# Graph layer kernel, the rows' stage: edge keys in four slices a group in place of one lump

## The chip, the core and the metric

The kernel runs on one core of one Trainium2 chip. Its engines run beside each other, each from its own instruction stream, and meet only at semaphores: PE (TensorE) multiplies and transposes into PSUM, DVE (VectorE) and ACT (ScalarE) do elementwise work, POOL (GpSimd) does some adds and issues indirect DMAs, SP issues plain DMAs. The metric is device time in microseconds (us). Three runs of the kernel before give a median of 2010.76 us, from 2009.63 to 2011.68.

## What is computed

One layer of a graph transformer on 6250 rows of 256 numbers: a two-layer graph convolution over 200000 edges plus self-loops, a linear attention ("mix") and a slice-token attention ("ffn"). Cut to what this case touches:

```python
edge_index = jnp.stack([src, dst])          # 200000 edges, sorted by dst, plus self-loops
xn = _layernorm(x)
x = x + gnn(xn, edge_index, W1, b1, W2, b2) + mix(xn[None], W_qkv, b_qkv, W_mo, b_mo)[0]
# in mix: q, k, v = split(xn @ W_qkv + b_qkv); q, k centred; q2 = q*q; k2 = k*k
# k2 = l2_normalize(k2 / (sum(k2) + 1e-7), over rows); q2 = l2_normalize(q2 / (sum(q2) + 1e-7), over columns)
x = x + ffn(_layernorm(x)[None], ...)[0]
```

## The kernel before

The rows are cut into T = 49 tiles of 128. The edges, sorted by their target row, are cut into windows of two target rows each. A window has up to 128 edge slots. A later stage builds the adjacency matrix from "keys": for each edge slot, `key_lo` holds the source row's place in its tile (source modulo 128) and `key_hi` holds the source's tile and which of the window's two rows the edge ends in.

The change lies in the **rows' stage** (lines 581 to 919), which runs from about 70 to 290 us. It walks over the 49 tiles, and for tile t:

- SP loads the rows of x (L637) and stores two transposed results (L640, L645).
- DVE, in its turn t, does in this order: `norm(t+1)` (L695 reciprocal, L699 normalised rows, L702 their f16 half), `stats(t+2)` (L687, L689, L690), `over_norm(t-2)` (L727, L729, L731, L733), `over_sums(t-1)` (L717, L719, L721), `halves(t+1)` (L707) and, in some turns, `edge_keys` (L673 to L682).
- PE, in its turn t: `project(t)` (L785, L787), `turn(t+1)`, which transposes the normalised rows (L776) and, in 28 turns, a piece of the keys first (`turn_keys`, L764), and `gather(t-2)` (L795, and L802, which transposes what L733 made).
- ACT, in its turn t: `low_keys` in some turns (L899), `norms(t-2)` (L877, L880, L883), `std(t+2)` (L856), `keep(t+1)` (L863), `squares(t)` (L872), `store_keys` in 28 turns (L905), `turned(t-3)` (L889).
- POOL, in its turn t: for the first 28 tiles one indirect DMA that gathers the sources of a quarter group's edges (L832), then an add of the k4 rows (L846), which waits for ACT's L883.

The keys come in G = 7 groups of WPS = 4 window rows each (112 partitions x 4 x 128 slots). Before, `edge_keys(g)` handles a whole group, 112x512, in one go, at the end of DVE's turns 10, 14, ..., 34 (`KEYS_LAG` = 10, each fourth tile). It takes five instructions: L673 the low seven bits, L674 which slots lie beyond the window's edges, L678 the shift by seven bits, L679 adding 1024 for slots beyond, L682 the high key. `low_keys(g)` on ACT turns the low bits into floats one tile later. `keyl` and `keyh` have two buffers each. PE transposes the keys in 28 turns from tile 13 on (`KEYS_TURN` = 13), and `parts_made`, `keys_made` and `keyl_ready` count the steps.

The order on each engine is the order in which these functions are called; no scheduler changes it. L699 waits, beside its own inputs, for a ring buffer of four that PE's L795 frees (`kx_done`), L764 and L776 wait for L699 (`xn_ready`), and L802 waits for L733 (`q2f_ready`).

Of the kernel before, what the change touches and what calls it, by code (L numbers as in the profile page):

```python
# [5 lines left out]
ALU = mybir.AluOpType  # L6
# [32 lines left out]
def gps_layer(nc, x, src, dst, W1, b1, W2, b2, W_qkv, b_qkv, W_mo, b_mo,  # L39
# [45 lines left out]
    with ExitStack() as life:  # L85
# [496 lines left out]
        with ExitStack() as stage:  # L582
# [8 lines left out]
            first = take([GW, G, WPS])  # L591
            second = take([GW, G, WPS, CAP])
            srcg = take([GW, G, WPS, CAP], I32)
            beyond = take([GW, WPS, CAP])
            src_lo = take([GW, 2, WPS, CAP], I32)
            keyl = take([GW, 2, WPS, CAP])
            keyh = take([GW, 2, WPS, CAP])
            take = carve(big_f[:, 0:KEYS_AT])
            x_in = take([P, RING, C])
            xn = take([P, RING, C + 2])  # L600
# [12 lines left out]
            nq = take([P, RING])  # L613
            fq = take([P, RING])
            before_sources = (16 * G, 16 * G, 0)
            KEYS_LAG, KEYS_TURN = 10, 13
            KEY_PARTS = 4 * G
            assert KEYS_TURN + KEY_PARTS < T and WPS == 4
            x_loaded = [sem(f"x_loaded{b}") for b in range(RING)]
# [35 lines left out]
            def _(dve):  # L655
# [7 lines left out]
                v.tensor_scalar(dun[:, :], dinv[:, :], 1.0 / SH, None, ALU.mult).then_inc(dinv_ready, 1)  # L663
                dve.wait_ge(dinv_ready, 2)

                def edge_keys(g):

                    r = g % 2
                    dve.wait_ge(gathered[g % 3], before_sources[g % 3] + 16 * WPS * (g // 3 + 1))
                    if g >= 2:  # L670
                        dve.wait_ge(keyl_ready, g - 1)
                        dve.wait_ge(xn_turned, KEYS_TURN + WPS * (g - 2) + WPS)
                    v.tensor_scalar(src_lo[:, r], srcg[:, g], P - 1, None, ALU.bitwise_and).then_inc(parts_made, 1)  # L673
                    v.tensor_tensor(beyond, slot.rearrange("p (o s) -> p o s", o=1).to_broadcast([GW, WPS, CAP]),  # L674
                                    many[:, g].rearrange("p (w o) -> p w o", o=1).to_broadcast([GW, WPS, CAP]), ALU.is_ge
                                    ).then_inc(parts_made, 1)
                    dve.wait_ge(parts_made, 4 * g + 2)
                    v.tensor_scalar(srcg[:, g], srcg[:, g], 7, None, ALU.logical_shift_right).then_inc(parts_made, 1)  # L678
                    v.scalar_tensor_tensor(out=second[:, g], in0=beyond, scalar=1024.0, in1=second[:, g],  # L679
                                           op0=ALU.mult, op1=ALU.add).then_inc(parts_made, 1)  # L680
                    dve.wait_ge(parts_made, 4 * g + 4)
                    v.scalar_tensor_tensor(out=keyh[:, r], in0=srcg[:, g], scalar=float(WIN), in1=second[:, g],  # L682
                                           op0=ALU.mult, op1=ALU.add).then_inc(keys_made, 1)

                def stats(t, b, u):
# [67 lines left out]
            def _(pe):  # L753
                te = nc.tensor

                def turn_keys(n, bank):

                    g, high, pair = n // WPS, n % WPS // 2, n % 2
                    if high:
                        pe.wait_ge(keys_made, g + 1)  # L760
                    else:
                        pe.wait_ge(keyl_ready, g + 1)
                    for j in range(2):
                        te.transpose(ps[:, bank, C + j * GW:C + (j + 1) * GW],  # L764
                                     (keyh if high else keyl)[:, g % 2, 2 * pair + j, :], ident[0:GW, 0:GW])

                def turn(t, b):
                    pe.wait_ge(xn_ready, t + 1)
# [55 lines left out]
            @block.gpsimd  # L824
            def _(pool):
                g = nc.gpsimd
                g.memset(k4_sum, 0.0).then_inc(k4_zeroed, 1)
                pool.wait_ge(k4_zeroed, 1)

                def gather_sources(g, j):  # L830

                    pool.indirect_dma_start(  # L832
                        out=srcg[:, g, j, :], out_offset=None, in_=src_dram.rearrange("(e a) -> e a", a=1),
                        in_offset=bass.IndirectOffsetOnAxis(ap=wlo[:, g, j:j + 1], axis=0)).then_inc(gathered[g % 3], 16)

                pool.wait_ge(src_padded, 32)

                def tile(t, b, u):
                    if t < WPS * G:
                        if t % WPS == 0 and t // WPS >= 3:  # L840
                            pool.wait_ge(parts_made, 4 * (t // WPS - 3) + 1)
                        gather_sources(t // WPS, t % WPS)
                    pool.wait_ge(k4_ready, 2 * t + 2)
                    if reached(t, 1):
                        pool.wait_ge(k4_added, t)
                    g.tensor_tensor(k4_sum[0:rows(t), :], k4_sum[0:rows(t), :], k4[0:rows(t), b, :], ALU.add).then_inc(k4_added, 1)  # L846

                pipeline(tile, T, RING)

            @block.scalar  # L850
            def _(act):
# [41 lines left out]

                def low_keys(g):

                    act.wait_ge(parts_made, 4 * g + 1)
                    if g >= 2:
                        act.wait_ge(xn_turned, KEYS_TURN + WPS * (g - 2) + 2)
                    a.copy(keyl[:, g % 2], src_lo[:, g % 2]).then_inc(keyl_ready, 1)  # L899

                def store_keys(t, b):

# [4 lines left out]
                           ps[:, 3 * (b % 2), C:C + 2 * GW].rearrange("p (j w) -> p j w", w=GW)).then_inc(keys_stored, 1)  # L907

                def tile(t, b, u):
                    if reached(t, KEYS_LAG + 1) and (t - KEYS_LAG - 1) % WPS == 0 and (t - KEYS_LAG - 1) // WPS < G:  # L910
                        low_keys((t - KEYS_LAG - 1) // WPS)
# [103 lines left out]
        def sum_edges(layer, halves, scratch, un):  # L1015
# [6 lines left out]
            with ExitStack() as stage:  # L1022
                block = stage.enter_context(nc.Block())

                @block.vector
                def _(dve):
                    nc.vector.tensor_tensor(acc[0:NT], halves[0:NT, :, 0:C], halves[0:NT, :, C:2 * C], ALU.add)
                    nc.vector.memset(key_lo[:, :], 0.0).then_inc(e_wide, 1)
# [953 lines left out]
```

## Time and profile before

| What | us |
|---|---|
| median of three runs | 2010.76 |
| the profiled execution's own time | 2019.06 |
| its span in the profile | 2017.1 |
| PE busy over the span | 1894.1 (94%) |
| DVE busy | 1185.0 (59%) |
| ACT busy | 852.7 (42%) |
| POOL busy | 300.0 (15%) |
| first and last start of L785, one for each of the 49 tiles | 75.5 and 280.7 |

The profile lists each instruction with its start, its duration, its engine, its line, and what it writes and reads by shape. Time in brackets is idle time of the engine just before it, and behind the arrow stands who released it. The start-to-start distance of two neighbours on an engine can be shorter than the first one's duration, because neighbours overlap. PEclk is the granted clock of TensorE as a share of full speed.

### The profile page before, as it was taken

How to read it: one execution, taken by the hardware profiler on the slowest of the kernel's cores; microseconds unless marked ns; L12 is line 12 of the kernel's file. 1: busy time of each engine (PE TensorE's matmuls, PEld its weight loads, DVE VectorE, ACT ScalarE, POOL GpSimd, SP SyncE). 2: the span in 40 equal slices, each digit the busy share in tenths (PEclk: the TensorE clock that was granted, in tenths of full speed). 3: DMA queues.
4: the chain of work that ended last, by engine and by line, in shares of the span. 5: the costliest groups of instructions: out<-in, count | busy, mean ns of one | idle time of the engine just before them, and what ended most of it. 6: DMA issues, size and time to landing. Idle time of an engine off the chain costs nothing. (4 is left out here: it accounts for less than half of the span.)

```text
span 2017.1 us, 45282 instructions
## 1 busy us (share of the span) xinstructions
PE 1894.1 (94%) x18843; PEld 1415.6 (70%) x18843; DVE 1185.0 (59%) x2748; ACT 852.7 (42%) x1970; POOL 300.0 (15%) x417
## 2 busy tenths in 40 slices
PE   3598989999999999999979999999999999999598
PEld 3254555555555555555559999999999999998476
DVE  6788887666666666666605555555555555555322
ACT  1577765665656665666602222222222222222100
POOL 3133110000000000000021111111111111111033
PEclk7698999999999999999989999999999999999599
DMA  3133322223232222223254444444444444442087
GB/s 97 51 108 94 93 74 104 121 97 129 97 129 97 122 104 109 117 97 129 96 187 142 144 144 144 144 140 144 143 143 143 144 143 143 142 142 78 13 269 241
DMA packets 92702, 252.13 MB, mean 125 GB/s; under 512 B 14143, under 2 KB 59347, under 8 KB 79939
## 3 DMA queue, kind: packets, MB, share of 16 engines
q1 hardware_dynamic: 69225, 218.83, 30.4%
q10 hardware_dynamic: 21096, 25.65, 3.6%
q0 software_dynamic: 2176, 4.75, 0.9%
q8 instruction: 150, 2.46, 0.5%
q14 instruction: 55, 0.44, 0.1%
HBM read 131.99 MB, written 118.02 MB: 124 GB/s over the span
## 5 line engine op out<-in xcount | busy, mean ns | idle before, releaser
L1392 PE MATMUL ps<-hs,at 128*128 128x512 f16 x2401 | 669.8, 379 | 0.3 <-POOL at L1209 0.3
L1611 PE MATMUL ps<-at,big 128*128 128x128 f16 x9604 | 576.8, 219 | 7.0 <-DMA at<-at_scratch 7.0
L1611 PEld LDWEIGHTS ps<-at,big 128*128 128x128 f16 x9604 | 555.7, 98 | 34.6 <-issue 8.4
L1448 ACT CAST at<-ps 128x392 f16<-128x392 f32 x784 | 375.0, 486 | 289.5 <-PE ps L1353 274.1
L1353 PE MATMUL ps<-big 128*128 128x98 f16 x3136 | 471.6, 208 | 8.1 <-DVE big L1293 8.1
L1353 PEld LDWEIGHTS ps<-big 128*128 128x128 f16 x3136 | 297.8, 98 | 142.6 <-DVE big L1293 9.7
L1392 PEld LDWEIGHTS ps<-hs,at 128*128 128x128 f16 x2401 | 230.1, 97 | 149.0 <-issue 1.8
L1293 DVE TENSOR_TENSOR big<-iota_lo,key_lo 128x1024 f16<-128x1024 f16 x392 | 268.2, 684 | 0.0
L1293 DVE TENSOR_TENSOR big<-iota_hi,key_hi 128x784 f16<-128x784 f16 x392 | 218.9, 559 | 1.1 <-PE ps L1353 1.0
L1725 DVE SCALAR_TENSOR_TENSOR big<-ps,small,blogb 128x512 f32<-128x512 f32 x49 | 36.8, 751 | 231.0 <-PE ps L1647 231.0
L1828 POOL TENSOR_TENSOR key_lo<-key_lo,big 128x512 f32<-128x512 f32 (+1 forms) x49 | 61.9, 1264 | 706.4 <-ACT big L1786 706.4
L1304 DVE TENSOR_TENSOR big<-ps,big 128x256 f32<-128x256 f32 x49 | 20.8, 425 | 198.1 <-ACT big L1456 198.1
L1209 POOL TENSOR_TENSOR at<-at,ident 128x120 f16<-128x120 f16 x98 | 30.0, 317 | 661.8 <-ACT at L1448 661.8
L1774 ACT ACTIVATE big<-big,eps 128x1 f32<-128x1 f32 x49 | 14.4, 295 | 224.0 <-DVE big L1710 224.0
L787 PE MATMUL ps<-at,big 128*128 128x512 f32 (+1 forms) x196 | 106.2, 667 | 0.0
L1776 ACT CAST big<-ps 128x512 f16<-128x512 f32 x49 | 28.7, 585 | 171.0 <-PE ps L1638 171.0
L977 PE MATMUL ps<-hs 128*128 128x256 f32 (+1 forms) x392 | 89.5, 390 | 7.3 <-DMA hs<-x_scratch 7.2
L1778 ACT ACTIVATE big<-big 128x512 f32<-128x512 f32 x49 | 30.8, 630 | 147.0 <-DVE big L1731 147.0
L977 PEld LDWEIGHTS ps<-hs 128*128 128x128 f32 (+1 forms) x392 | 75.0, 194 | 22.0 <-DMA hs<-x_scratch 11.3
L1696 DVE SCALAR_TENSOR_TENSOR big<-ps,dun,key_hi 128x256 f32<-128x256 f32 x49 | 23.7, 484 | 106.6 <-PE ps L1620 106.6
L1663 PE MATMUL ps<-big 128*128 128x256 f16 (+1 forms) x588 | 74.4, 278 | 0.0
L1647 PE MATMUL ps<-wlog,big 128*128 128x512 f16 x294 | 72.7, 384 | 0.7 <-ACT big L1776 0.7
(281 smaller groups left out, 2298.0 us busy)
## 6 DMA issues: line engine op xcount, KB each, us to landing
at_scratch<-at SPq DMA_DIRECT2D x49, 1568.0 KB, 5.2
at<-at_scratch SPq DMA_DIRECT2D x49, 1568.0 KB, 6.9
xT_scratch<-big SPq DMA_DIRECT2D x98, 128.0 KB, 2.0
big<-xT_scratch SPq DMA_DIRECT2D x49, 256.0 KB, 3.3
wT_scratch<-big ACTq DMA_DIRECT2D x49, 256.0 KB, 2.0
hs<-wT_scratch SPq DMA_DIRECT2D x49, 256.0 KB, 3.4
big<-in_x_dram SPq DMA_DIRECT2D x96, 128.0 KB, 2.4
x_scratch<-big ACTq DMA_DIRECT2D x48, 128.0 KB, 1.7
```

The lines of the kernel that those rows point to most:

```text
L787: mm = te.matmul(ps[0:rows(t), 1 + b % 2, :], lhsT=xt_now[:, b, c, 0:rows(t)], rhs=wqk[:, c, :], start=False, stop=(c == CB - 1))
L977: mm = nc.tensor.matmul(ps[0:rows(t), b, 0:C], lhsT=turned_in[:, b, i * NT:i * NT + rows(t)], rhs=w, start=(i == 0), stop=(i == len(weight ...
L1293: last = v.tensor_tensor(hot[:, s, :].rearrange("p (q k r) -> p q k r", k=width, r=2), iota.rearrange("p (o k) r -> p o k r", o=1).to_broa ...
L1353: te.matmul(ps[:, BANKS[i // UW % len(BANKS)], i % UW * KC:(i % UW + 1) * KC], lhsT=hot_lo[:, s, :].rearrange("p (q k r) -> p q k r", k=P, ...
L1392: mm = te.matmul(ps[:, 2 + b, :], lhsT=at[:, b, k * P:(k + 1) * P], rhs=hs[:, k, :], start=(k == 0), stop=(k == T - 1))
L1448: a.copy(to.rearrange("p k (i j) -> p k i j", j=WIN), ps[:, BANKS[m % len(BANKS)], 0:UW * KC].rearrange("p (i k j) -> p k i j", i=UW, j=WI ...
L1611: mm = te.matmul(ps[:, b, c * NT:(c + 1) * NT], lhsT=hs2[:, k, h * C + c * P:h * C + (c + 1) * P], rhs=at[:, b, k * P:(k + 1) * P], start= ...
L1647: mm = te.matmul(ps[0:NT, 4, :], lhsT=xn2T[:, b, xh, c * NT:(c + 1) * NT], rhs=wlog16[:, wh, c, :], start=(c == 0 and xh == wh == 0), stop ...
L1663: mm = te.matmul(ps[:, 6 + p // 2, (p % 2) * C:(p % 2 + 1) * C], lhsT=w_half[0:rows(t), b, p * P:(p + 1) * P], rhs=x_half[0:rows(t), b, :] ...
L1725: v.scalar_tensor_tensor(out=lg[0:NT, b].rearrange("p h d -> p (h d)"), in0=ps[0:NT, 4, :], scalar=unscale[0:NT], in1=blogb[0:NT, :], op0= ...
L1778: a.activation(ew[0:NT, b], lg[0:NT, b], ACT.Exp).then_inc(exp_ready, 1)
L1828: g.tensor_tensor(w_acc[:, :, 0:rows(t)], w_acc[:, :, 0:rows(t)], wt[:, b, :, 0:rows(t)], ALU.add).then_inc(w_added, 1)
```

## The change

- `edge_keys(g, j)` makes one quarter (112x128) of a group's keys. It is called at the end of each DVE turn from 8 to 35 (`KEYS_LAG` = 8), so 28 times with five instructions in place of 7 times with five.
- The second instruction compares against a scalar for each partition (`many[:, g, j]`), as a tensor_scalar, where it compared two tensors.
- `low_keys` on ACT stays one 112x512 conversion for each group, in turns 12, 16, ..., 36.
- `src_lo`, `keyl` and `keyh` have three buffers (`KEY_RING`) in place of two. The transposes start at tile 14 in place of 13.
- The semaphore counts of `parts_made` and `keys_made` follow: four times as many steps.
- In `sum_edges`, a path that runs only when some window has more than 128 edges, a memset of `key_lo` writes -1 in place of 0. The flag is not set for these inputs, and that path does not run.

```diff
-            beyond = take([GW, WPS, CAP])
-            src_lo = take([GW, 2, WPS, CAP], I32)
-            keyl = take([GW, 2, WPS, CAP])
-            keyh = take([GW, 2, WPS, CAP])
+            KEY_RING = 3
+            beyond = take([GW, CAP])
+            src_lo = take([GW, KEY_RING, WPS, CAP], I32)
+            keyl = take([GW, KEY_RING, WPS, CAP])
+            keyh = take([GW, KEY_RING, WPS, CAP])
...
-            KEYS_LAG, KEYS_TURN = 10, 13
+            KEYS_LAG, KEYS_TURN = 8, 14
...
-                def edge_keys(g):
-                    r = g % 2
-                    dve.wait_ge(gathered[g % 3], before_sources[g % 3] + 16 * WPS * (g // 3 + 1))
-                    if g >= 2:
-                        dve.wait_ge(keyl_ready, g - 1)
-                        dve.wait_ge(xn_turned, KEYS_TURN + WPS * (g - 2) + WPS)
-                    v.tensor_scalar(src_lo[:, r], srcg[:, g], P - 1, None, ALU.bitwise_and).then_inc(parts_made, 1)
-                    v.tensor_tensor(beyond, slot..., many[:, g]..., ALU.is_ge).then_inc(parts_made, 1)
+                def edge_keys(g, j):
+                    r, n = g % KEY_RING, 4 * (WPS * g + j)
+                    if j == 0:
+                        dve.wait_ge(gathered[g % 3], before_sources[g % 3] + 16 * WPS * (g // 3 + 1))
+                        if g >= KEY_RING:
+                            dve.wait_ge(keyl_ready, g - KEY_RING + 1)
+                            dve.wait_ge(xn_turned, KEYS_TURN + WPS * (g - KEY_RING + 1))
+                    v.tensor_scalar(src_lo[:, r, j], srcg[:, g, j], P - 1, None, ALU.bitwise_and).then_inc(parts_made, 1)
+                    v.tensor_scalar(beyond, slot, many[:, g, j:j + 1], None, ALU.is_ge).then_inc(parts_made, 1)
...
-                    if reached(t, KEYS_LAG) and (t - KEYS_LAG) % WPS == 0 and (t - KEYS_LAG) // WPS < G:
-                        edge_keys((t - KEYS_LAG) // WPS)
+                    if reached(t, KEYS_LAG) and (t - KEYS_LAG) // WPS < G:
+                        edge_keys((t - KEYS_LAG) // WPS, (t - KEYS_LAG) % WPS)
```

DVE at the end of its turns 8 and 9, where before no key work stood (the names in `big` are the stage's buffers; L707 ends a turn and L695 begins the next):

```order
+L675 TENSOR_SCALAR big<-big 112x128 [waits gathered0]
+L676 TENSOR_SCALAR big<-big 112x128
+L678 TENSOR_SCALAR big<-big 112x128 [waits parts_made]
+L679 SCALAR_TENSOR_TENSOR big<-big 112x128
+L682 SCALAR_TENSOR_TENSOR big<-big 112x128 [waits parts_made]
 L695 RECIPROCAL big<-big 128x1 [waits std_ready]
 L699 TENSOR_SCALAR big<-big 128x256 [waits kx_done,rstd_ready]
```

Five small instructions now stand ahead of L695 and L699, and the same five stand there in each of the 28 turns from 8 to 35.

DVE at the end of its turn 10, where the first lump stood:

```order
 L707 SCALAR_TENSOR_TENSOR hs<-big,dsc,hs 128x256 [waits hi_ready]
-L673 TENSOR_SCALAR big<-big 112x512 [waits gathered0]
-L674 TENSOR_TENSOR big<-big 112x512
-L678 TENSOR_SCALAR big<-big 112x512 [waits parts_made]
-L679 SCALAR_TENSOR_TENSOR big<-big 112x512
-L682 SCALAR_TENSOR_TENSOR big<-big 112x512 [waits parts_made]
+L675 TENSOR_SCALAR big<-big 112x128
+L676 TENSOR_SCALAR big<-big 112x128
+L678 TENSOR_SCALAR big<-big 112x128 [waits parts_made]
+L679 SCALAR_TENSOR_TENSOR big<-big 112x128
+L682 SCALAR_TENSOR_TENSOR big<-big 112x128 [waits parts_made]
 L695 RECIPROCAL big<-big 128x1 [waits std_ready]
```

The five 112x512 instructions are gone, and a quarter of them stands in their place.

ACT at the group conversion L899, which moves one turn later for the first group (L877 to L883 are `norms`, L856 is `std`):

```order
+L877 ACTIVATE big<-big 128x256 [waits recip_ready]
+L880 ACTIVATE big<-big 128x1 [waits k4_ready]
+L883 ACTIVATE big<-big 128x256 [waits k4_added]
+L856 ACTIVATE big<-big,eps 128x1 [waits ln_step]
+L863 COPY big<-ps 128x256 [waits x_out0,qk_ready,xn_turned]
+L872 ACTIVATE big<-ps 128x256 [waits k2n_ready,q2_turned,qk_ready]
+L872 ACTIVATE big<-ps 128x256
+L889 COPY big<-ps 128x256 [waits q_out0,q2_turned]
 L899 CAST big<-big 112x512 [waits parts_made]
```

A whole ACT turn now stands ahead of L899; it is still one 112x512 instruction for each group.

## Rows read from the trace of the kernel before

**Rows 1.** Stretches: us, busy us (instructions) by engine, granted clock, DMA share, GB/s

```profile
107.67:237.56 129.89, 116.59 (x413) 63.10 (x414) 113.30 (x428) 91.83 (x340) 42.26 (x49) 0.92 0.32 95
```

**Rows 2.** Timeline, PE: start us, duration us, engine, line, operation, tiles, idle before

```profile
159.50 0.41 PE L764 MATMUL ps<-ident,big 112*128 112x112 f32 x2 [1.88 <-DVE big L699]
...
161.88 0.60 PE L785 MATMUL ps<-at 3*128 3x512 bf16 x1
...
168.39 0.38 PE L785 MATMUL ps<-at 3*128 3x512 bf16 x1
...
172.13 0.38 PE L785 MATMUL ps<-at 3*128 3x512 bf16 x1
```

**Rows 3.** Waits, 107.67 to 237.56 us: us in total, times, longest

```profile
PE ps L764 <- DVE big L699: 10.0, 6, 1.9
DVE big L699 <- PE ps L795: 7.3, 3, 2.8
```

**Rows 4.** Stretches behind the first lump and behind the second

```profile
124.10:130.70 6.60, 6.60 (x16) 3.54 (x15) 3.52 (x17) 2.94 (x13) 1.66 (x2) 0.55 0.26 72
138.00:144.00 6.00, 4.24 (x18) 2.03 (x16) 5.65 (x19) 3.77 (x15) 2.27 (x3) 1.00 0.30 86
```

**Rows 5.** Timeline, DVE: the third lump and the instruction behind it

```profile
155.92 0.41 DVE L673 TENSOR_SCALAR big<-big 112x512 int32<-112x512 int32 x1
156.25 0.68 DVE L674 TENSOR_TENSOR big<-big 112x512 f32<-112x512 f32 x1
156.96 0.43 DVE L678 TENSOR_SCALAR big<-big 112x512 int32<-112x512 int32 x1
157.31 0.69 DVE L679 SCALAR_TENSOR_TENSOR big<-big 112x512 f32<-112x512 f32 x1
158.03 0.69 DVE L682 SCALAR_TENSOR_TENSOR big<-big 112x512 f32<-112x512 int32 x1
158.64 0.15 DVE L695 RECIPROCAL big<-big 128x1 f32<-128x1 f32 x1
```

**Rows 6.** Timeline, DVE, L699 alone: tiles 9, 37, 42 and 43

```profile
107.67 0.41 DVE L699 TENSOR_SCALAR big<-big 128x256 f32<-128x256 f32 x1
...
237.56 0.41 DVE L699 TENSOR_SCALAR big<-big 128x256 f32<-128x256 f32 x1
...
256.15 0.41 DVE L699 TENSOR_SCALAR big<-big 128x256 f32<-128x256 f32 x1
...
259.50 0.41 DVE L699 TENSOR_SCALAR big<-big 128x256 f32<-128x256 f32 x1
```

**Rows 7.** Groups by line and shape: busy us, mean ns, idle before

```profile
L1704 DVE SCALAR_TENSOR_TENSOR big<-big 128x256 f32<-128x256 f32 x49 | 20.8, 425 | 1.7
...
L1931 DVE TENSOR_SCALAR hs<-hs 128x128 f32<-128x128 f32 x4 | 0.9, 283 | 0.0
...
L340 DVE CAST ident<-ident 128x128 f16<-128x128 f32 x1 | 0.2, 219 | 0.0
```

**Rows 8.** Timeline, POOL's L846 and DVE: an ordinary tile, then behind a lump

```profile
153.69 0.73 POOL L846 TENSOR_TENSOR big<-big 128x256 f32<-128x256 f32 x1 [1.94 <-ACT big L883]
...
153.99 0.45 DVE L731 TENSOR_TENSOR big<-big 128x1 f32<-128x1 f32 x1
...
158.20 1.10 POOL L846 TENSOR_TENSOR big<-big 128x256 f32<-128x256 f32 x1 [2.70 <-ACT big L883]
...
158.83 0.62 DVE L699 TENSOR_SCALAR big<-big 128x256 f32<-128x256 f32 x1
```

**Rows 9.** Timeline: L699, ACT's L856 and POOL's L846 of one tile

```profile
141.31 0.62 DVE L699 TENSOR_SCALAR big<-big 128x256 f32<-128x256 f32 x1
...
142.91 0.29 ACT L856 ACTIVATE big<-big,eps 128x1 f32<-128x1 f32 x1 [2.19 <-DVE big L690]
...
146.17 0.72 POOL L846 TENSOR_TENSOR big<-big 128x256 f32<-128x256 f32 x1 [3.30 <-ACT big L883]
```

**Rows 10.** DMA issues, 80 to 290 us: the last number is the median us to landing

```profile
big<-src_scratch,big POOLq DMA_INDIRECT x27, 2.5
```

More of the change, by code:

```diff
@@ L664, in _ @@
                 dve.wait_ge(dinv_ready, 2)
-                def edge_keys(g):
-                    r = g % 2
-                    dve.wait_ge(gathered[g % 3], before_sources[g % 3] + 16 * WPS * (g // 3 + 1))
-                    if g >= 2:
-                        dve.wait_ge(keyl_ready, g - 1)
-                        dve.wait_ge(xn_turned, KEYS_TURN + WPS * (g - 2) + WPS)
-                    v.tensor_scalar(src_lo[:, r], srcg[:, g], P - 1, None, ALU.bitwise_and).then_inc(parts_made, 1)
[L674 to L679, printed above, removed]
+                def edge_keys(g, j):
[7 more added lines that the diff above has]
+                    v.tensor_scalar(beyond, slot, many[:, g, j:j + 1], None, ALU.is_ge).then_inc(parts_made, 1)
+                    dve.wait_ge(parts_made, n + 2)
+                    v.tensor_scalar(srcg[:, g, j], srcg[:, g, j], 7, None, ALU.logical_shift_right).then_inc(parts_made, 1)
+                    v.scalar_tensor_tensor(out=second[:, g, j], in0=beyond, scalar=1024.0, in1=second[:, g, j],
@@ L680, in edge_keys @@
                                            op0=ALU.mult, op1=ALU.add).then_inc(parts_made, 1)
-                    dve.wait_ge(parts_made, 4 * g + 4)
-                    v.scalar_tensor_tensor(out=keyh[:, r], in0=srcg[:, g], scalar=float(WIN), in1=second[:, g],
+                    dve.wait_ge(parts_made, n + 4)
+                    v.scalar_tensor_tensor(out=keyh[:, r, j], in0=srcg[:, g, j], scalar=float(WIN), in1=second[:, g, j],
                                            op0=ALU.mult, op1=ALU.add).then_inc(keys_made, 1)
@@ L759, in turn_keys @@
                     if high:
-                        pe.wait_ge(keys_made, g + 1)
+                        pe.wait_ge(keys_made, WPS * (g + 1))
                     else:
@@ L764, in turn_keys @@
                         te.transpose(ps[:, bank, C + j * GW:C + (j + 1) * GW],
-                                     (keyh if high else keyl)[:, g % 2, 2 * pair + j, :], ident[0:GW, 0:GW])
+                                     (keyh if high else keyl)[:, g % KEY_RING, 2 * pair + j, :], ident[0:GW, 0:GW])
                 def turn(t, b):
@@ L840, in tile @@
                         if t % WPS == 0 and t // WPS >= 3:
-                            pool.wait_ge(parts_made, 4 * (t // WPS - 3) + 1)
+                            pool.wait_ge(parts_made, 4 * WPS * (t // WPS - 3) + 1)
                         gather_sources(t // WPS, t % WPS)
@@ L894, in low_keys @@
                 def low_keys(g):
[L896 to L899, printed above, removed]
+                    act.wait_ge(parts_made, 4 * (WPS * g + WPS - 1) + 1)
+                    if g >= KEY_RING:
+                        act.wait_ge(xn_turned, KEYS_TURN + WPS * (g - KEY_RING) + 2)
+                    a.copy(keyl[:, g % KEY_RING], src_lo[:, g % KEY_RING]).then_inc(keyl_ready, 1)
                 def store_keys(t, b):
@@ L909, in tile @@
                 def tile(t, b, u):
-                    if reached(t, KEYS_LAG + 1) and (t - KEYS_LAG - 1) % WPS == 0 and (t - KEYS_LAG - 1) // WPS < G:
-                        low_keys((t - KEYS_LAG - 1) // WPS)
+                    if reached(t, KEYS_LAG + WPS) and (t - KEYS_LAG) % WPS == 0 and (t - KEYS_LAG) // WPS <= G:
+                        low_keys((t - KEYS_LAG) // WPS - 1)
                     if reached(t, 2) and within(t, T + 2):
@@ L1027, in _ @@
                     nc.vector.tensor_tensor(acc[0:NT], halves[0:NT, :, 0:C], halves[0:NT, :, C:2 * C], ALU.add)
-                    nc.vector.memset(key_lo[:, :], 0.0).then_inc(e_wide, 1)
+                    nc.vector.memset(key_lo[:, :], -1.0).then_inc(e_wide, 1)
                 @block.scalar
```

## The prediction

> **What bounds the kernel now.** I read the stage that the change touches first by its stretches, then PE's timeline, then the waits, then DVE's timeline. The change acts between L699 of tile 9 and L699 of tile 37, 107.67 to 237.56 us, 129.9 us for 28 turns or 4.64 us a turn [rows 6]. In it PE is busy for 116.6 us and DVE for 113.3 us [rows 1], so neither is idle for long, and the question is who waits for whom. A turn of PE that waits for nothing takes 172.13 - 168.39 = 3.74 us [rows 2]. A turn of DVE that waits for nothing takes 259.50 - 256.15 = 3.35 us [rows 6]. PE is therefore the bound in ordinary turns, and DVE has 0.4 us to spare. A lump of keys takes DVE 158.64 - 155.92 = 2.72 us [rows 5]. It eats that spare time and more. PE then stands 1.88 us at L764, waiting for L699 [rows 2], and such waits come to 10.0 us in 6 times [rows 3].
>
> There is a second loss. Behind the first lump the granted clock is 0.55 over a 6.6 us stretch in which PE never stops; behind the second it stays at 1.00 [rows 4]. The slow level shows in PE's pace too: the turn from 161.88 to 168.39 takes 6.51 us, 2.77 us more than 3.74 [rows 2]. It happened behind three of the seven lumps, 8.3 us in all, and DVE then waits for PE's L795 three times, 7.3 us [rows 3].
>
> **What the change takes away.** The seven lumps leave DVE: 7 x 2.72 = 19.0 us. PE's long waits go, and with them, if the clock then holds, the 8.3 us. The work itself is not what was lost: DVE's own turns and lumps are 28 x 3.35 + 19.0 = 112.8 us of the 129.9, which agrees with its 113.3 us busy [rows 1]. The other 17 us are waits, for the slow PE, for PE's 3.74 us pace in the turns between the lumps, and for POOL.
>
> **What it adds.** 28 slices, five instructions each, all on DVE and each with a start-up of its own. I cost a slice by start-to-start distances, since neighbours overlap. First instruction: L673 takes 0.41 and the next starts 0.33 behind it [rows 5]. An instruction of 128 columns of the same kind takes 0.219 (L340) [rows 7], 0.19 less, so 0.33 - 0.20 = 0.13. Second, now with a scalar: 0.283 by L1931 [rows 7]; the third waits for it, and such a wait adds 0.03 (0.71 from start to start for a duration of 0.68) [rows 5]: 0.31. Third: 0.35 - 0.21 = 0.14. Fourth: 0.69 at 512 columns [rows 5] and 0.425 at 256 [rows 7] make 1.02 ns a column, so 0.29 at 128, with the wait 0.32. Fifth: 0.61 from L682 to L695 [rows 5] less 384 x 1.02 ns = 0.22. The slice is 0.13 + 0.31 + 0.14 + 0.32 + 0.22 = 1.12 us. 28 of them are 31.4 us, 12.4 us more DVE work than the lumps. The bounds: a quarter of a lump, 0.68, if cost went by columns alone, and 0.22 + 0.28 + 0.22 + 0.29 + 0.29 = 1.30 if nothing overlapped. I take 1.12, as L673 to L682 do overlap.
>
> The Trainium skill (VectorE: DVE Perf Modes, the section on the TRN2 errata) speaks against this change: each SBUF instruction pays a fixed latency, so it advises tiles of at least 512 elements. By it the bound of 0.68 falls away, and with it a sum 12 us lower; the trace agrees (L340 with 128 columns takes more than half of L673's time with 512).
>
> **The new bound.** With a slice a DVE turn takes at least 3.35 + 1.12 = 4.47 us, over PE's 3.74. DVE sets the pace in all 28 turns, PE idles about 1 us in each, and nothing hides a DVE instruction any more. 28 x 4.47 = 125.2 us.
>
> **The collision with POOL.** While POOL's L846 runs, some DVE instructions stand still. In an ordinary tile L731, which works on one column, takes 0.45 us and ends with L846 at 154.4 [rows 8], where L695, also one column, takes 0.15 [rows 5]. It goes the other way too: behind a lump L846 takes 1.10 in place of 0.73, ending 0.58 after L682 did, and L699 then takes 0.62 in place of 0.41 and ends 0.15 after L846 [rows 5, 8]. So where L846 falls has a price. It follows L699 by 1.60 - 0.21 = 1.39 us (to ACT's L856, less L699's stretch) plus 3.26 us = 4.65 us [rows 9]. The next L699 comes at 4.47, so L846 arrives 0.18 us into it, waits for its end at 0.41, ends 0.58 later at 0.99, and L702 (alone done at 0.80) ends at 1.14: 0.34 us lost. In six of the turns ACT does the group conversion L899 first, which puts L846 half a microsecond later, onto L687 and L690, which I take as free of it: 0. In the first five intervals ACT has no keys to store yet and L846 falls on the slice's last instruction, as behind a lump: 0.21. Sum: 17 x 0.34 + 5 x 0.21 = 6.8 us. No row shows L702 being held, so its end of the range is 0, 5.8 us lower.
>
> The Trainium skill (SBUF — State Buffer, the section SBUF: two separate sides) calls this an exclusive lock held for a whole instruction, by DVE in a two-port mode or with two SBUF inputs, or by GpSimd. By it L702 would be held if it runs in such a mode, and the sum stays; if not, it would be 2007.1. The rows on L731 and L699 agree with a lock.
>
> **Edits with no cost.** ACT still makes seven conversions L899, a turn or two before their use, and at 4.6 us a turn it has over a microsecond to spare (91.8 busy of 129.9 [rows 1]). PE makes the same 28 transposes, one tile later; the extra one in the tail is under 0.3 us. The third buffer removes waits that no row shows. SP's queue and its 3 DMAs a tile are not passed by anything. POOL's gathers are now needed two turns earlier: the last of a group is issued about three turns before, and lands 2.5 us after [rows 10]. If that cover were gone, each late gather would stop DVE itself. The memset in `sum_edges` does not run.
>
> **Sum.** 125.2 + 6.8 = 132.0 us for the stretch, against 129.9: **+2.1 us**. The profiled execution took 2019.06 us, 8.3 more than the median of the runs; I expect the same difference, so 2021.2 in the profile and 2010.76 + 2.1 = **2012.9** as the median.
>
> **Rival 1: slices cost their full durations.** A slice is 1.30 and not 1.12, because small instructions with semaphores between them don't overlap, or because the gather's or POOL's work holds them. 28 x 0.18 = 5.0 us more: 2017.9, slower. For it: L674 and L679 are followed only after their full duration [rows 5]. Against it: L673, L678 and L682 are not. It decides from a slice of 1.19 on, where the sum passes +4 us. The Trainium skill (VectorE: DVE Perf Modes, The DRAIN you can't avoid) says that the next instruction doesn't start until the pipe is empty, which would give this time; rows 5 disagree for three of five.
>
> **Rival 2: the clock drops.** PE idles in every turn, about 1.0 us of 4.7, in two pieces (at L764 for L699, at L802 for L733). If that were enough to lose the full clock throughout, a turn would be 6.51 us [rows 2], 28 x 6.51 = 182.3, so +52 and 2063. Against it: the drop followed one wait of 1.88 us, and behind the second lump, where PE was busy for 4.24 of 6.00 us, it didn't come [rows 4].
>
> **Rival 3: the gain that the change looks for.** No wait for POOL: 125.2 us, -4.7, so 2006.1. A cheaper slice too, 1.0: -8. With 0.68 it would be 28 x 4.03 = 112.8, -17 and 1993.7, the far bound. For it: L702's price is not shown. Against it: L731 is held in ordinary tiles, so some collision is likely wherever L846 falls.
>
> **Rival 4: it doesn't do what it says**, because a gather lands late or the group conversion on ACT holds `norms` and through it L727. Up to 0.6 us in seven turns, +4: 2017.
>
> **How the numbers follow.** Within 0.2% is about what a measurement of this kernel can tell from no change, 4.0 us, or 2006.7 to 2014.8. Forecast 0.58, of which 0.43 within, 0.14 slower, 0.01 faster (0.1 us of error in a slice is 2.8 us). Rival 1 0.18 (0.15 slower, 0.03 within), rival 2 0.04, rival 3 0.17 (0.12 faster, 0.05 within), rival 4 0.03. Together: faster 0.13, same 0.51, slower 0.36. The range takes in rivals 1 and 4 above and most of rival 3 below, and leaves out rival 2 and the far bounds: 2005.5 to 2021.0.
>
> **What the profile after would show.** The interval between two L699 about 4.5 to 4.8 us from tile 10 to 37 with no idle time on DVE; a slice of 1.12 from its first instruction to L695; PE waiting in each turn at L764 and L802, together 1 us; PEclk 1.00 throughout the stretch; L846 drawn out to about 0.8 and L702 to 0.69. I am wrong on the slice if it takes under 1.0 or over 1.2, wrong on the collision if L702 stays at 0.35, and wrong on the clock if PEclk falls in the stretch.

## The result: 2018.0 us, 0.35% slower, and what the profile after shows

| | before | after |
|---|---|---|
| median of 6 runs each | 2010.95 us | 2017.99 us |
| lowest to highest | 2009.63 to 2016.32 | 2016.91 to 2019.79 |
| profiled execution, its span | 2019.06, 2017.1 | 2018.20, 2016.4 |
| stretch from L699 of tile 9 to L699 of tile 37 | 129.89 | 132.50 |

The ratio is 1.0035 with an interval of 1.0021 to 1.0049. The forecast was 2012.9, with the best chance on a time within 0.2% of before. The time lies within the stated range of 2005.5 to 2021.0, but 5.1 us above the forecast, and the interval of the ratio lies just outside those 0.2%. The profile of the changed kernel looks almost as foretold. What failed is the step from the profile to the median.

The stretch of after, in the columns of [rows 1] (stretch, its length, busy us and instructions of PE, PEld, DVE, ACT and POOL, granted clock, DMA share, GB/s):

```profile
105.35:237.85 132.50, 116.82 (x414) 56.16 (x414) 122.50 (x532) 90.29 (x340) 41.84 (x49) 1.00 0.31 94
```

Against [rows 1], DVE has 9.2 us more, and the clock is 1.00 where it was 0.92. PE is busy for 117 us both times, but that is chance: [rows 1] holds the slow turns, and at a clock of 1.00 the kernel before has 107.17 (its repeat, below). The same multiplications overlap less when each waits for its input. The forecast for this stretch was 132.0.

DVE's timeline of after, a slice and the first instructions behind it (start, duration, as in [rows 5]):

```profile
179.71 0.22 DVE L675 TENSOR_SCALAR big<-big 112x128 int32<-112x128 int32 x1
179.84 0.28 DVE L676 TENSOR_SCALAR big<-big 112x128 f32<-112x128 f32 x1
180.16 0.23 DVE L678 TENSOR_SCALAR big<-big 112x128 int32<-112x128 int32 x1
180.31 0.28 DVE L679 SCALAR_TENSOR_TENSOR big<-big 112x128 f32<-112x128 f32 x1
180.62 0.29 DVE L682 SCALAR_TENSOR_TENSOR big<-big 112x128 f32<-112x128 int32 x1
180.83 0.16 DVE L695 RECIPROCAL big<-big 128x1 f32<-128x1 f32 x1
181.03 0.41 DVE L699 TENSOR_SCALAR big<-big 128x256 f32<-128x256 f32 x1
```

From 179.71 to 180.83 it is 1.12 us, in steps of 0.13, 0.32, 0.15, 0.31 and 0.21. The prediction had 1.12, in steps of 0.13, 0.31, 0.14, 0.32 and 0.22.

DVE and POOL behind it, where L846 of one tile meets L702 of a later one:

```profile
185.54 0.41 DVE L699 TENSOR_SCALAR big<-big 128x256 f32<-128x256 f32 x1
...
190.36 0.41 DVE L699 TENSOR_SCALAR big<-big 128x256 f32<-128x256 f32 x1
190.81 0.70 DVE L702 TENSOR_SCALAR hs<-big,dsc 128x256 f16<-128x256 f32 x1
...
190.54 0.82 POOL L846 TENSOR_TENSOR big<-big 128x256 f32<-128x256 f32 x1 [2.91 <-ACT big L883]
```

L846 starts 0.18 us into L699, ends at 191.36, which is 0.59 after L699 ended at 190.77, and L702 ends 0.15 behind it, at 191.51. In a turn without the meeting L702 takes 0.35. From 185.54 to 190.36 the turn takes 4.82 us, with an L702 of 0.70 in it too; the one before it, 181.03 to 185.54, takes 4.51, since ACT's group conversion came first and L846 fell beside L687. From its seventh turn on the stretch repeats this pattern, three turns of 4.81 and one of about 4.5, and L702 is held in 17 turns, as forecast.

PE's waits in the stretch, after (what waits, for what: us in total, times, longest):

```profile
PE ps L802 <- DVE big L733: 13.9, 27, 0.6
PE ps L776 <- DVE big L699: 0.7, 3, 0.2
PE ps L764 <- DVE big L699: 0.2, 1, 0.2
```

One turn of PE, from L787 to L802, with the weight load of L764 (PEld):

```profile
183.99 1.98 PE L787 MATMUL ps<-at,big 128*128 128x512 f32 x4
186.01 0.20 PEld L764 LDWEIGHTS ps<-ident,big 112*128 112x128 f32 x2 [0.86 <-DVE big L699]
186.01 0.41 PE L764 MATMUL ps<-ident,big 112*128 112x112 f32 x2
...
188.12 0.44 PE L802 MATMUL ps<-ident,big 128*128 128x128 f32 x2 [0.61 <-DVE big L733]
```

The six long waits at L764 of [rows 3] are gone, and so are DVE's waits for a slow PE. In their place PE waits 0.5 us in nearly each turn, at L802. The wait records don't hold all of what PE loses: L764's weight load stood 0.86 us for L699, and L764 itself starts 2.02 us behind L787, where in the repeat of before, in a turn without a wait, it starts 1.82 behind. A turn of 4.81 us is 1.07 longer than PE's own 3.74.

### The profile page after: what moved, and what is told of

Read it like the earlier page. It is cut to its first block and busy times, and to the rows that moved or that the text cites. A ratio compares the mean times of both kernels' runs of the same rounds, so it can differ in the third digit from the quotient of the medians.

```text
span 2016.4 us, 45385 instructions
## 1 busy us (share of the span) xinstructions
PE 1891.2 (94%) x18843; PEld 1408.2 (70%) x18843; DVE 1193.9 (59%) x2853; ACT 850.9 (42%) x1970; POOL 299.9 (15%) x417
## 5 line engine op out<-in xcount | busy, mean ns | idle before, releaser
L787 PE MATMUL ps<-at,big 128*128 128x512 f32 (+1 forms) x196 | 99.0, 628 | 0.0
```

Source lines behind the costliest of these rows:

```text
L787: mm = te.matmul(ps[0:rows(t), 1 + b % 2, :], lhsT=xt_now[:, b, c, 0:rows(t)], rhs=wqk[:, c, :], start=False, stop=(c == CB - 1))
```

## The experiments

All ratios are to the kernel before on the same chip. Line numbers behind an edit move by a few lines.

### Was the profiled execution before a typical one?

The profiled execution of before was 8.3 us above the median, and three slow turns in it cost just that. So the kernel before was run again, unchanged.

> The kernel before, once more. In question: the median rose by 7.0 us, but the profiled executions differ by -0.9 us (2019.06 before, 2018.20 after) and the changed stretch by only +2.6 us (129.9 to 132.5). Theory A: the profiled execution of before is not a typical one; the three turns at the slow clock (8.3 us) are rare in its ordinary executions, whose stretch is then near 122 us. It expects a mean granted clock of most executions near 0.967, against 0.963 in the profiled one, and a span near 2009 us. Theory B: the slow turns are typical, and the changed kernel loses time somewhere else in the kernel when it isn't the one profiled; it expects 0.963 in most executions here too, with a time near 2011 us.

Measured: 2009.12 us (median of 12, 2006.48 to 2018.85), ratio 1.0003. The profiled execution took 2007.38, with a span of 2005.6. Its stretch, in the columns of [rows 1], with the piece behind its first lump (the answer to [rows 4]), and PE's waits:

```profile
107.65:229.04 121.39, 107.17 (x413) 58.82 (x414) 112.85 (x427) 92.49 (x340) 42.47 (x49) 1.00 0.34 102
124.10:130.70 6.60, 6.60 (x27) 3.96 (x27) 6.06 (x27) 5.00 (x20) 2.58 (x4) 1.00 0.38 121
```

```profile
PE ps L764 <- DVE big L699: 10.6, 6, 1.9
PE ps L802 <- DVE big L733: 2.0, 7, 0.5
PE ps L776 <- DVE big L699: 1.6, 1, 1.6
```

PE waits at the lumps as long as in [rows 3], 10.6 us in 6 times and up to 1.9. Yet the clock stays at 1.00 behind the first lump, where [rows 4] has 0.55. The stretch is 121.4 us, and 129.9 less the three slow turns of 8.3 is 121.6. The same program loses the clock behind some lumps in one execution and behind none in another.

In this stretch of 121.4 us the profile lists not one wait of DVE, for PE or anyone else. So DVE, and not PE, sets its length, also in the ordinary turns between lumps. Here is such a turn:

```profile
162.93 0.41 DVE L699 TENSOR_SCALAR big<-big 128x256 f32<-128x256 f32 x1
...
164.30 0.72 POOL L846 TENSOR_TENSOR big<-big 128x256 f32<-128x256 f32 x1 [1.98 <-ACT big L883]
...
164.56 0.48 DVE L731 TENSOR_TENSOR big<-big 128x1 f32<-128x1 f32 x1
...
166.71 0.41 DVE L699 TENSOR_SCALAR big<-big 128x256 f32<-128x256 f32 x1
```

It takes 3.78 us. That is near PE's 3.74, but what makes it longer than 3.35 is mostly L731, held until L846 ends (both at 165.0): 0.48 for the 0.16 that it takes in the experiments below. The kernel before pays for POOL too.

The other executions fit this. Of 97 of the kernel before, 55 had a mean granted clock of 0.967 or more, with a median of 2008.5 us; 24 had 0.966, with 2011.5; 18 had 0.965 or less, with 2013.6. All 97 together have a median of 2010.4. The clock does not fix the time in each single one (the ranges overlap), but the order is clear. That it is the slow turns of this stretch which lower the mean clock was seen in profiled executions alone. The changed kernel, run again, tests it from the other side:

> The changed kernel once more, beside the kernel before on the same chip. Theory: its stretch has no slow turns in any execution, so its executions lie close together at a granted clock of 0.968 or more, 2015 to 2020, median 2017 to 2018.5; the kernel before has two groups, and against the one without slow turns (near 2008) the change costs 9 to 11 us. Rival: the spread of the kernel before has nothing to do with the stretch, and the changed kernel shows the same spread of 10 us.

Measured: 2017.18 us (median of 7, 2015.96 to 2018.77), ratio 1.0034 (1.0022 to 1.0047); the stretch takes 132.44 us at a clock of 1.00, and all 13 executions of the changed kernel have a mean clock of 0.968 to 0.971. So the comparison of like with like is 132.5 to 121.4 in the stretch, 11.1 us. The executions that the stretches of after and of the repeat come from agree: 2018.20 - 2007.38 = 10.8. The spread of 10 us did not come, and so the rival is out as it was put. But slow turns are not the only source of spread: the two variants of the changed kernel below, with L846 narrow or moved, spread over 5.8 and 7.3 us at mean clocks of 0.967 or more.

### Does PE's standstill at the lumps cost the clock?

Before, with four small multiplications on PE ahead of its wait for L699 in the seven turns that have a lump. Their result is not used.

```
 def turn(t, b):
+    if t >= KEYS_LAG + 2 and (t - KEYS_LAG - 2) % WPS == 0 and (t - KEYS_LAG - 2) // WPS < G:
+        for i in range(4):
+            te.matmul(ps[:, 6 + b % 2, C:2 * C], lhsT=ident[:, :], rhs=wqk[:, 0, 0:C], start=True, stop=True)
     pe.wait_ge(xn_ready, t + 1)
```

> The kernel before, with PE kept at work in the seven turns in which it waits for a lump: four extra multiplications of 128x256 (about 1.7 us at full clock), whose results go to columns of PSUM that nobody reads, stand ahead of its wait for L699. Theory: the slow turns come from PE standing still there; with the filler the clock stays at 1.00 throughout the stretch in all executions, the executions of 2011 us and more go, and the median is 2006 to 2009. Rival: the clock falls for another reason, and the spread of 2005 to 2017 stays, or the filler delays PE by more than it saves (0.2 us in each lump, 1.5 us).

Measured: 2006.73 us (median of 11), ratio 0.9983 (0.9972 to 0.9994). No execution is above 2009.20, where before's reach 2015.39 on the same chip. The stretch (columns as in [rows 1]), and PE's timeline at a lump with the added work, L770:

```profile
105.33:226.78 121.45, 118.92 (x469) 69.34 (x470) 112.90 (x428) 92.64 (x340) 42.59 (x49) 1.00 0.34 102
```

```profile
117.61 1.89 PE L770 MATMUL ps<-at,ident 128*128 128x256 f32 x8
119.36 0.44 PE L779 MATMUL ps<-ident,big 128*128 128x128 f32 x2
```

PE now works through the 1.9 us in which it stood. The stretch is as long as in the repeat of before, 121.45 and 121.39, since DVE still sets it. So the 4.4 us under before's median on this chip (2011.11) are not a shorter stretch; the executions with slow turns are gone. Extra work on an engine that waits paid for itself.

### The collision with POOL: L846 made narrow

After, with L846 on one column in place of 256.

```
-g.tensor_tensor(k4_sum[0:rows(t), :], k4_sum[0:rows(t), :], k4[0:rows(t), b, :], ALU.add)
+g.tensor_tensor(k4_sum[0:rows(t), 0:1], k4_sum[0:rows(t), 0:1], k4[0:rows(t), b, 0:1], ALU.add)
```

> The changed kernel with POOL's add L846 on one column in place of 256 (the sums of k4 are left out but for one column). Theory: in 17 turns L846 holds DVE's L702 for 0.35 us and in 5 turns L699 for about 0.2 us. Without it L702 stays at 0.35 in all turns, the interval of two L699 is 4.47 us in all 28 turns, and the stretch from L699 of tile 9 to that of tile 37 is 125 to 126 us in place of 132.5, the time 6 to 7 us below the changed kernel's 2018.0. Rival: L702 is long for another reason (the slice's instructions or DMA traffic), and stretch and time stay within 1 us.

Measured: 2010.50 us (median of 10), ratio 1.0002 (0.9992 to 1.0013), 7.5 below after. The stretch:

```profile
106.66:231.75 125.09, 116.89 (x416) 56.48 (x415) 115.10 (x532) 90.87 (x343) 27.26 (x49) 1.00 0.33 100
```

125.09 is what the prediction has without the collision, 28 x 4.47 = 125.2, and every turn takes 4.46 to 4.49. The collision costs 132.50 - 125.09 = 7.4 us; the prediction had 6.8.

### The same with all the work kept: L846 moved out of the way

After, with one wait more on POOL. `hi_ready` counts the finished L702, so L846 now starts behind L702 and runs beside L687, L690 and the small instructions.

```
 pool.wait_ge(k4_ready, 2 * t + 2)
+pool.wait_ge(hi_ready, min(t + 5, T))
```

> The changed kernel, with one wait added: POOL starts its add L846 of tile t only after DVE's L702 of tile t+4, so that it runs beside L687, L690, L727 and L729, which the rows show to be free of it. Theory: the wait for POOL is a matter of where L846 falls. L702 and L699 keep their own durations, L731 too, the interval of two L699 is 4.47 us in all 28 turns, the stretch 125 to 126 us, the time 6 to 7.5 us below the changed kernel, 2010.5 to 2012, with all of L846's work done. Rival: the wait delays ACT (through the ring of four k4 buffers) or POOL's gathers, and DVE then waits for them; less than 3 us of gain.

Measured: 2010.29 us (median of 10), ratio 0.9996 (0.9985 to 1.0007), 7.7 below after (6.9 below its repeat, which ran on the same chip). The stretch, and one turn of DVE and POOL (L847 is the old L846):

```profile
104.33:229.57 125.24, 116.91 (x417) 56.49 (x415) 115.24 (x533) 90.90 (x343) 41.01 (x50) 1.00 0.33 100
```

```profile
185.33 0.35 DVE L702 TENSOR_SCALAR hs<-big,dsc 128x256 f16<-128x256 f32 x1
...
186.51 0.16 DVE L731 TENSOR_TENSOR big<-big 128x1 f32<-128x1 f32 x1
...
185.82 0.72 POOL L847 TENSOR_TENSOR big<-big 128x256 f32<-128x256 f32 x1 [2.67 <-ACT big L884]
```

L702 takes 0.35 again and L731 0.16, where [rows 8] has 0.45 for L731. Both experiments give the same stretch, so the collision is a matter of place alone, and it is the whole of what lies over 4.47 a turn.

### Fewer instructions in a slice

After, with the slice cut to three instructions: L676 and L679 are left out.

```
-v.tensor_scalar(beyond, slot, many[:, g, j:j + 1], None, ALU.is_ge).then_inc(parts_made, 1)
-v.scalar_tensor_tensor(out=second[:, g, j], in0=beyond, scalar=1024.0, in1=second[:, g, j],
-                       op0=ALU.mult, op1=ALU.add).then_inc(parts_made, 1)
```

> The changed kernel with three instructions in a slice in place of five: the comparison with the number of edges and the adding of 1024 (L676, L679) are left out, so slots beyond a window's edges are not marked. Theory (DVE sets the pace, each slice costs its start-to-start distances): 0.31 + 0.32 us less in each of 28 turns, 17.7 us, so a DVE turn of 3.84 us before any wait for POOL and a stretch of 108 to 117 us; time 2000 to 2003. Rival (PE's reaction or the wait for POOL sets the pace, DVE's instructions are hidden): less than 9 us of gain.

Measured: 2007.73 us (median of 10), ratio 0.9988 (0.9978 to 0.9998), 10.3 below after, with a stretch of 120.5 us. Both are above what the theory gave (117 us at most, 2003 at most). DVE's timeline shows the slice (the last instruction is now L679):

```profile
137.18 0.22 DVE L675 TENSOR_SCALAR big<-big 112x128 int32<-112x128 int32 x1
137.44 0.23 DVE L677 TENSOR_SCALAR big<-big 112x128 int32<-112x128 int32 x1
137.70 0.29 DVE L679 SCALAR_TENSOR_TENSOR big<-big 112x128 f32<-112x128 int32 x1
137.91 0.15 DVE L692 RECIPROCAL big<-big 128x1 f32<-128x1 f32 x1
```

It takes 137.91 - 137.18 = 0.73 us, and 0.49 was expected. In the full slice L676 starts 0.13 behind L675, since it needs nothing from it; here each instruction needs the one ahead and follows after 0.26. Taking out two instructions saves 0.39 and not 0.63. The shortest turns take 4.07 us, which is 3.35 + 0.73; the others, 4.19 to 4.62, meet L846 in new places (L699 takes up to 0.96, L702 up to 0.89). So start-up decides, as the prediction said, but an instruction that fills another's latency is cheaper to keep than its duration tells.

### Halves in place of quarters

After, with 14 halves (112x256), one each second turn.

```
-r, n = g % KEY_RING, 4 * (WPS * g + j)
+r, n, w = g % KEY_RING, 4 * (2 * g + j), slice(2 * j, 2 * j + 2)
...
-if reached(t, KEYS_LAG) and (t - KEYS_LAG) // WPS < G:
-    edge_keys((t - KEYS_LAG) // WPS, (t - KEYS_LAG) % WPS)
+if reached(t, KEYS_LAG) and (t - KEYS_LAG) // WPS < G and (t - KEYS_LAG) % 2 == 0:
+    edge_keys((t - KEYS_LAG) // WPS, (t - KEYS_LAG) % WPS // 2)
```

> The changed kernel with halves: 112x256 in each second turn from 8 to 34, 14 times five instructions, the rest as changed. By the same start-to-start distances a half is 0.20 + 0.45 + 0.21 + 0.45 + 0.35 = 1.66 us, so two DVE turns are 2 x 3.35 + 1.66 = 8.36 us against PE's 7.48. Theory: the stretch is 14 x 8.36 = 117 us plus 2 to 5 us of waits for POOL, 119 to 122 us, no drop of the clock, and the time is 10 to 13 us below the changed kernel, 2005 to 2008. Against the kernel before that is a gain of 3 to 6 us. Rival: a half makes PE wait long enough to lose the full clock behind some of the 14, 2.8 us each, and the gain goes.

Measured: 2011.54 us (median of 10), ratio 1.0013 (1.0003 to 1.0023), 6.5 below after; the stretch is 125.71 us, where the expectation ended at 122, and the time 3.5 us over its upper end of 2008. A half takes 1.66 us as worked out, but two turns take 9.0 us in place of 8.36. DVE and POOL in two turns that follow each other (L735, L701 and L848 are the old L733, L699 and L846):

```profile
142.90 0.74 DVE L735 TENSOR_SCALAR big<-big 128x256 f32<-128x256 f32 x1
...
142.76 0.73 POOL L848 TENSOR_TENSOR big<-big 128x256 f32<-128x256 f32 x1 [3.83 <-ACT big L885]
...
146.47 0.62 DVE L701 TENSOR_SCALAR big<-big 128x256 f32<-128x256 f32 x1
...
146.01 0.93 POOL L848 TENSOR_TENSOR big<-big 128x256 f32<-128x256 f32 x1 [1.44 <-ACT big L885]
```

The old L733 takes 0.74 for 0.35 and the old L699 0.62 for 0.41: L846 has found other victims. Each new rhythm of DVE puts it somewhere else. If that is the whole difference, halves with the wait of the experiment before must come to their arithmetic.

> The kernel with 14 halves, with the same added wait of POOL. In the kernel with halves two turns took 9.0 us, 0.65 more than the 8.36 of its start-to-start sum, because L846 falls on L731 or L733 in one turn and on L701 in the other. Theory: with the wait two turns take 8.36 us, the stretch is 117 to 118 us, and the time is 8 us below the halves' 2011.5, 2003 to 2004.5; that is 6 us under the kernel before and beats both. Rival: PE's wait behind each half (1 us) together with less DVE time lets the clock fall in some executions, and the median stays above 2007.

Measured: 2003.32 us (median of 8), ratio 0.9965 (0.9953 to 0.9976), stretch:

```profile
106.92:224.64 117.72, 110.34 (x414) 58.18 (x413) 108.62 (x462) 90.14 (x341) 41.03 (x50) 1.00 0.35 106
```

Turns take 5.01 (some up to 5.16) and 3.35 us, which is 3.35 + 1.66 and 3.35; two are 8.36, and 14 x 8.36 = 117.0. The theory holds.

### The lumps with POOL out of the way

The kernel before, with the same one wait, and nothing of the change.

> The kernel before, lumps and all, with the same added wait of POOL. Theory: PE is the bound between lumps, so freeing L731 there hides; the lumps get 0.2 us (L699) cheaper and DVE catches up in 3.35 us turns. Stretch of an execution without slow turns 118 to 120.5 in place of 121.4 us; slow turns come as before, so the median falls by 1 to 3 us. Rival: POOL's collision is worth as much here as in the changed kernel, and the time falls by 6 us or more.

Measured: **2000.99 us** (median of 6, 1998.85 to 2002.57), ratio 0.9949 (0.9935 to 0.9962), the fastest version that computes everything: 10 us under before, 17 under after. The stretch, PE's wait at the lumps, and one turn:

```profile
107.36:223.52 116.16, 107.69 (x415) 59.43 (x415) 105.60 (x427) 91.04 (x343) 41.03 (x50) 1.00 0.36 107
```

```profile
PE ps L764 <- DVE big L699: 5.8, 6, 1.0
```

```profile
120.97 0.35 DVE L702 TENSOR_SCALAR hs<-big,dsc 128x256 f16<-128x256 f32 x1
121.23 0.42 DVE L687 BATCH_NORM_STATS2 big<-big 128x6 f32<-128x256 f32 x1
...
122.14 0.16 DVE L731 TENSOR_TENSOR big<-big 128x1 f32<-128x1 f32 x1
...
121.45 0.73 POOL L847 TENSOR_TENSOR big<-big 128x256 f32<-128x256 f32 x1 [4.27 <-issue]
```

L847 now lies on L687 and what follows it; L687 takes 0.42, L731 0.16. Four turns take 6.55 + 3.35 + 3.35 + 3.39 = 16.6 us, and in the repeat of before 6.46 + 3.56 + 3.72 + 3.78 = 17.5. The ordinary turns are now at DVE's 3.35, PE waits less at a lump (1.0 us, not 1.9), and its clock held in every execution (means of 0.969 to 0.972). My theory gave 1 to 3 us, the rival 6 or more, and the rival was right. The theory failed where it had PE as the bound between lumps. PE's own turns are 3.74 us here too, yet DVE's ordinary turns fell from 3.56, 3.72 and 3.78 to 3.35, 3.35 and 3.39: DVE runs ahead of PE between two lumps and spends the lead on the next lump. What is taken off any DVE turn therefore shortens the stretch. Whether the collision is the whole of it was tested by the narrow L846 on the kernel before:

> The kernel before with POOL's add L846 on one column (the sums of k4 are left out but for one column). The added wait in the kernel before brought a stretch of 116.2 us and 2001.0 us. Theory: that gain is the collision with L846 and nothing else, so with hardly any L846 the stretch is the same 116 us within 1 us, no slow turns, and the time 1999 to 2003. Rival: the added wait helped by pacing ACT or the gathers; then this kernel stays above 2004 and its stretch above 118.

Measured: 2000.44 us (median of 5), ratio 0.9959 (0.9942 to 0.9975), stretch 115.78 us. It is the same gain with the collision removed in the other way. The five executions spread from 1996.53 to 2004.48, one of them with a mean clock of 0.966, so that the clock held in all of them is not shown here. Of the 10 us of the added wait, 121.39 - 116.16 = 5.2 lie in the stretch, and they are all of the difference between the two profiled executions (spans of 2005.6 and 2000.5 us). Another 2 to 3 may be the slow turns that no longer come (2011.1 is the median of before here, 2008.5 that of its executions with a mean clock of 0.967 or more). The remaining 2 to 3 us are not settled.

### The third buffer and the lags alone

Before, with three buffers of `keyl` and `keyh`, transposes from tile 14, and the lumps one turn later. `src_lo` keeps two: beside the full-size `beyond`, which the change makes a quarter as large, a third would need 12500 columns of the stage's 12288. The waits follow (not shown).

```
-keyl = take([GW, 2, WPS, CAP])
-keyh = take([GW, 2, WPS, CAP])
+KEY_RING = 3
+keyl = take([GW, KEY_RING, WPS, CAP])
+keyh = take([GW, KEY_RING, WPS, CAP])
...
-KEYS_LAG, KEYS_TURN = 10, 13
+KEYS_LAG, KEYS_TURN = 11, 14
```

> The kernel before with the rest of the change and not the slices: three buffers of keyl and keyh (src_lo keeps two, for space), transposes from tile 14 on, the lumps in turns 11, 15, ..., 35, still whole groups of 112x512. Theory: buffers and lags cost and bring nothing, a stretch of seven lump groups as long as before (four turns 17.5 us without slow turns), time as before, 2007 to 2012, with the same two groups of executions. Rival: the buffers or the later start are worth something of their own (more than 3 us either way).

Measured: 2009.51 us (median of 10), ratio 1.0004 (0.9990 to 1.0017). The buffers and the later start are worth nothing that ten executions can tell from zero. Its profiled execution, 2008.72 us, gives a second look at slow turns; 28 turns with all seven lumps (L699 of tile 11 to that of tile 39), and the two slow ones:

```profile
112.19:238.73 126.54, 113.45 (x415) 61.87 (x416) 113.27 (x427) 92.03 (x340) 40.49 (x47) 0.95 0.32 97
158.30:165.10 6.80, 6.80 (x16) 3.21 (x15) 5.16 (x22) 3.62 (x14) 1.66 (x2) 0.50 0.27 77
195.80:202.60 6.80, 6.80 (x16) 3.19 (x15) 5.05 (x22) 3.62 (x14) 0.72 (x1) 0.50 0.24 70
```

Here two lumps of seven cost the clock, which is at half speed behind them, at 158 and at 196 us; in the profile of before it was three, and in its repeat none.

## Why the prediction was right in its parts and wrong in its sum

- **What bounds the kernel**: half wrong. DVE's turn of 3.35 and PE's of 3.74 are right as durations: the shortest turns of every variant are 3.35 us plus its key work. But PE is not "the bound in ordinary turns", and DVE did not have 0.4 us to spare there. Without slow turns DVE never waits in the stretch of before, and its ordinary turns fall to 3.35 once L846 is out of the way. Of the 17 us that the prediction put down to waits, 8.5 are the slow turns (129.89 - 121.39), 5.2 to 5.6 are L846 holding DVE (to 116.16 and 115.78), and some 3 remain, of which the runs don't show the cause. No wait of DVE for PE is listed but the three behind slow turns. That 112.8 us of DVE work "agrees with" 113.3 us busy hid this. The busy time counts an instruction that is held, and leaves out the gaps between instructions; with L846 moved the same work is busy for 105.60.
- **The slice at 1.12 us**: right, each step within 0.01. (The first step took 0.20 off where its own figures give 0.19, and 1.02 ns a column where they give 1.04; neither moves the sum by more than 0.02.) Rival 1, 1.30 us, is refuted, though its 2017.9 is the time that was measured: that is chance. The small instructions do overlap, where they don't need each other's result.
- **DVE sets the pace, 28 x 4.47 = 125.2**: right. The two variants without the collision have stretches of 125.09 and 125.24.
- **The collision, +6.8**: right in mechanism and place, 7.3 to 7.4 in size. L702 was forecast at 0.69 and takes 0.70, though no row of before showed it being held. The first two intervals were not as forecast in detail (4.66 and 4.93). The Trainium skill (SBUF — State Buffer, the section SBUF: two separate sides) has whichever starts first of such a DVE instruction and a GpSimd one hold the shared ports for the whole instruction; the trace agrees, with L702 ending 0.15 us behind L846.
- **Where PE waits**: right. I had about 1 us a turn, at L764 and L802. A turn of 4.81 us is 1.07 over PE's own, though the wait records show only 14.8 us in the stretch, 0.53 a turn, nearly all at L802. The forecast clock, 1.00 throughout, came, so rival 2 is out.
- **"The profiled execution took 2019.06 us, 8.3 more than the median of the runs; I expect the same difference"**: this is the step that failed. The rows showed both numbers side by side: 8.3 us over the median, and three slow turns of 2.77, together 8.3. That is not a constant difference between a profile and a median. It is what made this one execution unusual. I let the change remove the slow turns within the stretch (129.9 to 132.0), and then took their 8.3 us off again for the median. After's own profile is 0.2 above its median. Without slow turns the stretch of before is 121.4, so against it my own 132.0 is +10.6, and the runs have +11.1. The median of before, 2010.76, stands 3.4 above the execution without slow turns (2007.38), since it lies between executions with them and such without. So the term "+2.1" should have stood near 10.6 - 3.4 = +7.2; measured is +7.0.
- **Rival 3, no wait for POOL**: its 125.2 us for the stretch is right if L846 is moved or narrowed, but the change does neither. Its 2006.1 suffers from the same error; the two variants took 2010.3 and 2010.5. Rival 4 did not come: no PE or DVE wait for a gather shows.

So the change put 31.4 us of slices in the place of 19.0 us of lumps, 12.4 more, on the engine that set the pace before and after. POOL's holds are not new: they cost 7.3 to 7.4 us where they cost 5.2 to 5.6 before. Against that, some 3 us of small waits of before are gone. That makes the 11.1. What the change removes beside them is PE's waits at the lumps, which cost nothing by themselves as DVE sets the length, and slow turns that only some executions have.

## What to carry to other kernels

When a profiled execution is far from the median, find the rows that carry the difference before using it, and never count them once in the sum and once in the step to the median. Spreading a lump over turns helps only if the engine that does it has room over the whole period. Here a period of four turns was 4 x 3.35 + 2.72 = 16.1 us of DVE and 4 x 3.74 = 15.0 of PE, so DVE had none, and four slices cost 4.48 where the lump cost 2.72. One turn alone, 3.35 against 3.74, made it look otherwise. And look for a DVE instruction that lasts twice its usual time beside one on POOL: one wait that moved the POOL instruction was worth more than any division of the work.

## What the hardware showed that I had not expected

- **The clock behind the same wait is not always the same.** Six or seven waits of up to 1.9 us in an execution cost the full clock three times, twice or never (129.89, 126.54 and 121.39 us for stretches of 28 turns), about 2.8 us each. With PE filled by spare multiplications, or with its waits cut to 1.0 us by the added wait of POOL, the mean clock of every execution stayed at 0.968 or more. With the narrow L846, where its waits are as short, one of five had 0.966. What decides whether a wait costs the clock is open.
- **POOL's add of 256 columns holds up some DVE instructions and not others.** L702 goes from 0.35 to 0.70, L733 from 0.35 to 0.74, L699 from 0.41 to 0.62, and L731, of one column, from 0.16 to 0.48, while the statistics L687 stay at 0.41 to 0.42 beside it.
- **The start of the stage moves by itself.** PE's third L785 starts at 85.96 us in the profile of before, at 83.63 in that of after, and at 85.55 in after's repeat, all ahead of any instruction that the change touches. So the stretch of after starts at 105.35 us and that of its repeat at 107.27, which is no merit of the change. It hardly shows in the whole: their spans are 2016.4 and 2016.8 us.
